# A second layer in six fp32r products, moved behind the fourth expert layer, in a graph and feed-forward kernel

## What is computed

```python
def _shared_mlp(x, W1, b1, W2, b2, W3, b3):
    h = jax.nn.relu(x @ W1 + b1)        # 256 -> 256
    h = jax.nn.relu(h @ W2 + b2)        # 256 -> 128
    return h @ W3 + b3                  # 128 -> 256
...
all_out = _experts_mlp(x, eW1, eb1, eW2, eb2, eW3, eb3)   # four experts: 256 -> 128 -> 64 -> 256
shared = _shared_mlp(x, sW1, sb1, sW2, sb2, sW3, sb3)
gates = jax.nn.softmax(x @ gW + gb, axis=-1)
topv, topi = jax.lax.top_k(gates, TOPK)                   # two of four
topw = jax.nn.softmax(topv, axis=-1)
...
return shared + gated
```

## Time and profile before

| | |
|---|---|
| time, median of 3 runs | 2529.49 us (2528.87 to 2534.21) |
| time of the profiled execution | 2531.6 us |
| its span | 2529.8 us |
| TensorE busy over the span | 2203.3 us (87%) |
| VectorE busy | 1877.0 us (74%) |
| ScalarE busy | 1331.9 us (53%) |
| GpSimd busy | 1180.6 us (47%) |

### The profile page before, as it was taken

One profiled execution on the slowest core, in us unless ns is written; L12 is line 12 of the kernel. 1 busy time (PEld: TensorE's weight loads), 2 busy tenths in 40 slices (PEclk: granted clock), 3 DMA queues, 4 the chain that ended last, 5 costly groups with the idle time before them and its releaser, 6 DMA issues.

```text
span 2529.8 us, 78810 instructions
## 1 busy us (share of the span) xinstructions
PE 2203.3 (87%) x29478; PEld 1816.5 (72%) x29502; DVE 1877.0 (74%) x5694; ACT 1331.9 (53%) x2860; POOL 1180.6 (47%) x940
## 2 busy tenths in 40 slices
PE   5777787898889889889998988988788899999999
PEld 2566566687878768878877878877787566666666
DVE  9876886777778678888765667665798677766775
ACT  2677677655556666566566556655000444444443
POOL 0667775566566566666666566566000111111110
PEclk7989998999999999999999999999999899999999
DMA  2333443566666546666655566664676011111111
GB/s 73 98 108 111 153 131 118 161 178 182 202 204 187 183 154 187 188 203 204 190 174 169 174 189 207 198 189 145 198 212 195 30 57 57 57 57 40 55 57 34
DMA packets 251783, 361.19 MB, mean 143 GB/s; under 512 B 35216, under 2 KB 225354, under 8 KB 250222
## 3 DMA queue, kind: packets, MB, share of 16 engines
q1 hardware_dynamic: 207972, 236.08, 33.5%
q0 software_dynamic: 43200, 119.22, 12.9%
q10 hardware_dynamic: 234, 0.85, 0.1%
HBM read 208.01 MB, written 197.15 MB: 160 GB/s over the span
## 4 chain that ended last, share of the span: by engine, by line
PE 71%; issue 9%; ACT 6%; DVE 5%; DMA 4%; another core or an unknown queue 3%; DVEq 1%; POOL 1%; SPq 0%; ACTq 0%; POOLq 0%
PE bank L676 17%; PE moved L647 16%; PE bank L763 9%; PE bank L633 7%; PE moved L776 6%; PE bank L651 4%; DMA arena<-table 3%; PE bank L660 2%; ACT arena L1436 2%; ACT arena L1442 2%; PE bank L803 2%; PE bank L601 1%; PE bank L727 1%; DMA table<-arena 1%
## 5 line engine op out<-in xcount | busy, mean ns | idle before, releaser
L1640 POOL DMA_INDIRECT table<-arena x832 | 1048.6, 1260 | 663.4 <-ACT arena L1442 390.5
L1442 ACT ACTIVATE arena<-moved 128x588 bf16<-128x588 f32 x832 | 546.2, 661 | 269.7 <-PE moved L647 173.6
L647 PE MATMUL moved<-arena 128*128 128x196 bf16 x4992 | 616.1, 259 | 35.4 <-ACT arena L1442 18.0
L1436 ACT ACTIVATE arena<-bank 128x512 f32<-128x512 f32 x624 | 372.5, 597 | 356.6 <-remote 169.6
L647 PEld LDWEIGHTS moved<-arena 128*128 128x128 f16 x4992 | 462.2, 100 | 127.9 <-issue 38.9
L1097 DVE TENSOR_TENSOR sums<-sums,bank 128x130 f32 x960 | 274.3, 286 | 323.9 <-PE bank L676 225.4
L1176 DVE TENSOR_TENSOR arena<-arena 128x3072 f16<-128x3072 f16 x208 | 364.5, 1753 | 48.3 <-PE moved L647 28.3
L676 PE MATMUL bank<-arena,w_all 128*128 128x64 bf16 (+1 forms) x8640 | 348.1, 195 | 56.0 <-issue 46.8
L676 PE MATMUL bank<-arena 128*128 128x64 bf16 (+1 forms) x8640 | 346.3, 195 | 56.8 <-issue 36.8
L676 PEld LDWEIGHTS bank<-arena 128*128 128x128 bf16 x8640 | 313.6, 99 | 73.2 <-issue 54.5
L676 PEld LDWEIGHTS bank<-arena,w_all 128*128 128x128 bf16 x8640 | 313.5, 99 | 72.6 <-issue 64.2
(11 more groups left out here) (234 smaller groups left out, 2604.4 us busy)
## 6 DMA issues: line engine op xcount, KB each, us to landing
arena<-table SPq DMA_DIRECT2D x320, 441.0 KB
arena<-in_attr SPq DMA_DIRECT2D x208, 144.0 KB
table<-arena POOLq DMA_INDIRECT x832
x_ln<-arena SPq DMA_DIRECT2D x98, 128.0 KB
arena<-in_x SPq DMA_DIRECT2D x97, 128.0 KB
arena<-x_ln SPq DMA_DIRECT2D x24, 512.0 KB, 4.7
out_rows<-arena SPq DMA_DIRECT2D x24, 512.0 KB, 3.3
fused_node<-arena SPq DMA_DIRECT2D x98, 32.0 KB
```

Of the source, the lines that this page charges most:

```text
L647: mm = e.matmul(moved8[:, 4 * (n % 2) + h, 0:PW], slot_hot[s % NSLOT][:, t, h * P:(h + 1) * P], upper(s, 0, PW)[:, t, :], start=j == 0, st ...
L1436: return e.activation(part_of_pay(s, c0, A), z, ACT.Relu)
L1442: e.activation(row_buf[n % NROWS], moved8[:, 4 * (n % 2):4 * (n % 2) + 3, 0:PW], ACT.Copy).then_inc(s_rows, 1)
L1640: e.indirect_dma_start(out=tables[k], out_offset=bass.IndirectOffsetOnAxis(ap=dest[s % NDEST][:, a:a + 1], axis=0), in_=row_buf[n % NROWS] ...
```

## The change

The second shared layer h2 is computed as `layer1` does it: six fp32r products (`second`) instead of two float32 matmuls. Three pieces of work are new for that. VectorE masks h1 into `h1_top` and writes the low half, two and two instructions of 512 columns, placed right behind the copies into w5. ScalarE copies `h1_top` into the high half, two instructions placed behind the relu of e2_0. And w2 is split once by VectorE, in three instructions behind the first mean. TensorE now does h2 behind e1_3, and the sum of h2 with w3 behind the transposes of xn; the bias rows open the sum in the output banks. The relu of h2 moves behind that of e1_3. `held` takes the new halves in words that were free, so no buffer of another use is shared.

```diff
+        s_w2, s_h1_top, s_h1_high, s_h1_low = sem("s_w2"), sem("s_h1_top"), sem("s_h1_high"), sem("s_h1_low")
...
+        h1_halves = [held[:, (2 + i) * K * TN * P:(3 + i) * K * TN * P].rearrange("p (k t) -> p k t", k=K) for i in range(2)]
+        w2_halves = [held[:, 4 * K * TN * P + i * K * SH2:4 * K * TN * P + (i + 1) * K * SH2].rearrange("p (k m) -> p k m", k=K) for i in range(2)]
...
-        U = {name: i for i, name in enumerate(("h1_0", "h1_1", "e1_0", "e1_1", "h2", "e1_2", "e2_0", "e1_3", "e2_1"))}
+        U = {name: i for i, name in enumerate(("h1_0", "h1_1", "e1_0", "e1_1", "e1_2", "e2_0", "e1_3", "h2", "e2_1"))}
...
+            def second(g):
+                w = nt[g] * P
+                u = hid_no(g, "h2")
+                e.wait_ge(s_hid, u - 2)
+                e.wait_ge(s_w2, 3)
+                e.wait_ge(s_h1_high, K * (g + 1))
+                e.wait_ge(s_h1_low, K * (g + 1))
+                terms = [(k, a, b) for k in range(K) for a, b in ((0, 0), (1, 0), (0, 1))]
+                for i, (k, a, b) in enumerate(terms):
+                    mm = e.matmul(bank[BH[(u - 1) % 2]][:, 0:w], w2_halves[a][:, k, :], h1_halves[b][:, k, 0:w], start=i == 0, stop=i == len(terms) - 1)
+                mm.then_inc(s_hid_ps, 1)
...
                     layer1(h, "e1_1", lambda a, k: we1[a][:, 1, k, :])
                     w = nt[h] * P
-                    u = hid_no(h, "h2")
-                    e.wait_ge(s_hid, u - 2)
-                    for k in range(K):
-                        mm = e.matmul(bank[BH[(u - 1) % 2]][:, 0:w], w2[:, k, :], h1[:, k, 0:w], start=k == 0, stop=k == K - 1)
-                    mm.then_inc(s_hid_ps, 1)
...
                     layer1(h, "e1_3", lambda a, k: we1[a][:, 3, k, :])
-                    e.wait_ge(s_hid, hid_no(h, "h2"))
+                    second(h)
                     if h:
                         e.wait_ge(s_o, h)
-                    final(h, h2, w3, True, False)
-                    final(h, w5_t, b3_r[:], False, False)
+                    final(h, w5_t, b3_r[:], True, False)
                     expert2(h, 1)
...
                     mm.then_inc(s_y_ps, 1)
                 if heavy:
+                    e.wait_ge(s_hid, hid_no(h, "h2"))
+                    final(h, h2, w3, False, False)
                     final(h, e2[:, 0, :], we3[:, 0, :], False, False)
...
             mean(0)
+            w2_flat = w2.rearrange("p k m -> p (k m)")
+            e.tensor_scalar(w2_top.bitcast(i32), w2_flat.bitcast(i32), HIGH_BITS, None, ALU.bitwise_and).then_inc(s_w2, 1)
+            e.wait_ge(s_w2, 1)
+            e.tensor_copy(w2_halves[0].rearrange("p k m -> p (k m)"), w2_top).then_inc(s_w2, 1)
+            e.tensor_tensor(w2_halves[1].rearrange("p k m -> p (k m)"), w2_flat, w2_top, ALU.subtract).then_inc(s_w2, 1)
...
                     ins.then_inc(s_w5, 1)
+                    w = n * P
+                    for k in range(K):
+                        e.wait_ge(s_hid, hid_no(h, f"h1_{k}"))
+                        if h:
+                            e.wait_ge(s_h1_high, K * (h - 1) + k + 1)
+                        e.tensor_scalar(h1_top[:, k, 0:w].bitcast(i32), h1[:, k, 0:w].bitcast(i32), HIGH_BITS, None, ALU.bitwise_and).then_inc(s_h1_top, 1)
+                    if h:
+                        e.wait_ge(s_hid_ps, hid_no(h - 1, "h2"))
+                    for k in range(K):
+                        e.wait_ge(s_h1_top, K * h + k + 1)
+                        e.tensor_tensor(h1_halves[1][:, k, 0:w], h1[:, k, 0:w], h1_top[:, k, 0:w], ALU.subtract).then_inc(s_h1_low, 1)
                 if light:
...
-                    if h:
-                        e.wait_ge(s_out_ps, h)
-                    relu(h, "h2", h2, b_2)
                     relu(h, "e1_2", e1[:, 2, :], b_e1[:, 2:3])
...
                     relu(h, "e2_0", e2r[:, 0, :], b_e2[:, 0:1])
+                    if h:
+                        e.wait_ge(s_hid_ps, hid_no(h - 1, "h2"))
+                    for k in range(K):
+                        e.wait_ge(s_h1_top, K * h + k + 1)
+                        e.activation(h1_halves[0][:, k, 0:n * P], h1_top[:, k, 0:n * P], ACT.Copy).then_inc(s_h1_high, 1)
                     relu(h, "e1_3", e1[:, 3, :], b_e1[:, 3:4])
+                    if h:
+                        e.wait_ge(s_out_ps, h)
+                    relu(h, "h2", h2, b_2)
                     relu(h, "e2_1", e2r[:, 1, :], b_e2[:, 1:2])
```

More of the change, by code:

```diff
@@ L299, in gnn_ffn @@
         h2 = carve([TN * P], f32)
+        w2_top = carve([K * SH2], f32)
+        h1_top = carve([K, TN * P], f32)
         e1 = carve([E_, TN * P], f32)
```

## The result

The changed kernel took 2568.59 us (median of 5 runs, 2561.53 to 2570.73), the kernel before 2534.21 us in the runs taken beside it (2528.87 to 2555.69). The ratio is 1.0124 with a 95% interval of 1.0088 to 1.0159: some 31 us slower (the medians differ by 34.4). The forecast was 2567.7 us in a range of 2558 to 2581, and slower with 0.94.

The account below looks back on a forecast made before the run. TensorE looked full, but a second loop through VectorE had 2.24 us slack; 2.0 + 1.73 added, 0.15 for wake-up, made 1.64 us more a group. With the ends 38.2 us on 2529.49: 2567.7 us, range 2558 to 2581.

Parts of the forecast that it names:

- VectorE's loop: Gate transposes, VectorE's gate chain, x1, statistics, xn, then TensorE's transposes back to gate transposes; slack 2.24 us a group.
- Step 2: VectorE's two masks and two subtractions of h1 between w5 and x1: 2.0 us a group, 2.23 at most.
- Step 5: Loop after the change: x1 to xn, wait of some 1.3 us, transposes; a group takes 24.01 us, 1.64 more.
- Step 4: ScalarE's two copies behind the relu of e2_0: six products wait 0.3 us; TensorE reaches the xn transposes at about 2304.1.
- Step 1: TensorE's old h2 layer (1.72 us) replaced by six products (1.39): 0.33 us less a group, about 8 us in all.
- the sign that I named for it: In the changed profile, TensorE's busy time was to go down 8 us while the span grows.
- Step 6: Ends: first interval +1.0 us, last norm group +0.3, last heavy group +0.8; 22 steady groups 36.1; sum 38.2.
- The clock rival: New pauses on TensorE lower its granted clock in each group, 40 us on top, about 2608 us; chance 0.05.
- The faster rival: TensorE stays the bound and the kernel gains 8 us, 2521.5 us; chance 0.04.

Follow-up runs that it names:

- e3: Kernel before with both the moved sum of h2 and w3 and the unused split of h1, float32 h2 product kept; node stage 568.5 us (+29.7), ratio 1.0145.
- e4: Changed kernel with the sum of h2 and w3 back ahead of the transposes of xn; node stage 549.6 us, ratio 1.0045 to the kernel before.
- e6: Changed kernel with each VectorE mask of h1 made twice, second result unused; node stage 583.8 us, 15.1 more than the change.
- e1: Kernel before with only the sum of h2 and w3 moved behind the transposes of xn; node stage 549.2 us (+10.4), ratio 1.006.
- e11: e9 with the fused rows' relu and the gate gap's exponential ahead of e1_0's relu on ScalarE; 2245.21 us against 2250.03 before, ratio 0.9982.
- e2: Kernel before with only the split of h1 (masks, subtractions, copies) added, results unused; node stage 539.6 us (+0.8), ratio 0.9989.
- e7: Changed kernel with the sum of h2 and w3 moved on behind the gate transposes; node stage 555.8 us, ratio 1.0071 to the kernel before.
- e9: Changed kernel with the h2-w3 sum behind the gate transposes, ScalarE's copies ahead of e1_2's relu, fusion one layer earlier; node stage 559.1 us, ratio 1.0098.
- e5: Changed kernel with ScalarE's two copies moved ahead of the relu of e1_2; node stage 568.9 us, 0.2 from the change, ratio 1.0142 to the kernel before.

## Why the prediction held, and where it was off

The direction, the mechanism and the time were right: the split and the moved sum together use up the slack of VectorE's loop, and the six products change nothing that shows. e3, e4 and e6 each confirm one piece. But the size of the growth was not right. The medians agree to a microsecond (2567.7 forecast, 2568.59 measured) by luck, since the kernel before came out at 2534.21 in the comparison and not at 2529.49; the profiled execution, for which I had 2569.8, took 2561.53. By the traces the node stage grew by 30.1 us, where I had 38.2. The 8 us lie in the steady group: 1.25 us instead of 1.64 takes 8.6 us off in 22 of them, the two long groups put 0.6 back, and the ends nearly cancel.

- **Step 2, the four new instructions, is the term that was mis-sized.** I added 2.0 us to the start of x1. Measured from the gate arithmetic, x1 moved from 8.98 to 10.70, 1.72. Of the 0.28 missing, 0.12 is the work itself, 1.88 us from the first mask (2480.87) to x1 (2482.75). About 0.10 is slack I did not see: before, the last w5 copy started at 2297.49 and x1 0.18 later, while now the next instruction follows 0.08 later. The reason, read from the traces: x1 also needs the up projection L812, which in that group starts at 2296.49 and takes 1.13 us, so it ends at 2297.62, and x1 starts 0.05 later. In e1 x1 stands 0.27 behind the last w5 copy (2306.25), and again 0.05 behind the end of L812 (2305.34 + 1.13), at 2306.52. I counted a wait of x1 in the first group only. The remaining 0.06 lies in the gate chain, which took 8.74 instead of 8.80 up to that copy.
- **Step 5.** The statistics and the power took 4.21 instead of 4.27: before, xn stood behind the product of e2_0, which waited for ScalarE; now only the power counts. From xn to the transposes 1.44 was measured where I had 1.53 with the wake-up; the piece behind them was 6.86 instead of 6.81. A group came to +1.25 by the timeline instead of +1.64.
- **Step 4** held within 0.2 us: the wait for the copies was 0.37 in the bracket and 0.54 from start to start (L788 at 2484.37, the product before it at 2483.61, where an unblocked step is 0.22; 0.3 forecast), TensorE reached the transposes 15.97 us behind the gate transposes (one step of 0.22 after the spread at 2487.39; 15.83 forecast). It waited 0.79 us from there to their start and not 1.3, because xn came earlier.
- **Step 1** held: TensorE's saving was real and showed in e11 as 0.34 us a group. But the sign that I named for it did not come. TensorE's busy time did not fall by 8 us; over the span it rose from 2203.3 to 2206.8, and a steady group's from 22.3 to 22.5 (486.77 and 465.54 of 489 us). The likely reason, not tried: a matmul's busy time has its last results in it, and next to a pause these overlap with nothing. The step from start to start is the sign to name.
- **Step 6.** The first interval grew by 1.33 us (forecast 1.0), the last by 0.42 (0.3), the end behind the last logit maximum by 0.2 (0.8). The six half-width products fell on the exposed end (0.93 us, 2551.65 to 2552.58), but the sum of h2 with w3 now ran at the full clock, while before it ran in the slow stretch.
- **The clock rival** did not come. With pauses of 0.37 and 0.62 us in each group the granted clock of the steady stretch is 1.00.
- **The faster rival** needed VectorE's loop to keep its slack. With either piece alone it keeps some (in e2 no transposes wait, and in e1 xn is ready 0.93 us ahead of them); with both it has none.

## What to carry to other kernels

Beside the engine that is full, look for the loop that returns to it through another engine, and measure its slack in us from one start to the next; a share of 71% on VectorE said nothing of the 2.24 us that it really had. Two pieces of work can each fit into the slack (one cost 0.8 us alone, the other 10.4, and those through another wait) and cost 30 us together, so a change is to be costed against the slack that the rest of it leaves. And when work is moved, ask both what it pushes back and what it had covered: three of the misses here (e1, e7, e9) were such a neighbour's wait, and each showed by name in the changed trace.

## What the hardware showed that I had not expected

TensorE's clock bore more than I had allowed. In e5 it waited 1.4 us in every steady group, and the granted clock of the stretch from 2000 to 2400 us was still 1.00. In the last group of the changed kernel TensorE stood for 3.38 us, and then the granted clock was 0.50, the 1.2 GHz level, for the two us that follow; both in the view by stretches and the timeline of the changed kernel:

```profile
2549.00:2551.00 2.00, 2.00 (x11) 1.24 (x12) 1.03 (x5) 1.07 (x4) 0.00 (x0) 0.50 0.16 53
...
2553.00:2556.50 3.50, 3.37 (x17) 2.32 (x17) 0.52 (x2) 0.79 (x2) 0.00 (x0) 1.00 0.00 0
```

```profile
2548.93 0.30 PE L832 MATMUL bank<-ident_bf,arena 128*45 128x128 bf16 x1 [3.38 <-DVE arena L1339]
```

Between 2551 and 2553 it was 0.76 and from 2553 on 1.00 again. TensorE was busy throughout those four us at a mean of 0.63, so an estimate of the price is 4 x 0.37 = 1.5 us. In the last group of the kernel before, a pause of 1.70 us went ahead of such a stretch; in e5 one of 1.4 did not bring one.

Neighbouring VectorE instructions overlap a little more than I took: two masks of 512 columns, 424 ns each alone, start 0.335 us apart (2480.87 to 2481.54 for two), and the two subtractions, 692 ns alone, 0.605 us apart (2481.54 to 2482.75). And the edge stage, which none of the edits touches, differed far more between chips (250 us between the second and the third set of runs) than anything tried here; only the comparison on one chip, or the stage alone, could decide.
